# FFN weights transposed by VectorE instead of TensorE, and a new written-out order from pair 26 to the end of an attention plus FFN kernel

## The chip, the cores and the metric

The kernel runs on one core of a Trainium2 chip. Its metric is the device time of one execution in microseconds. Engines are named as in the profile: PE is TensorE's matmul stream, PEld its weight loads, DVE is VectorE, ACT is ScalarE, POOL is GpSimd, SP is SyncE, which here only issues DMAs.

## The reference, cut to what matters

A gated cross-attention layer is followed by a gated feed-forward layer (FFN), all in float32. `x` and `ctx` are 8 batches of 128 tokens with 512 features.

```
def _L0_xattn_ref(query, key, value, ...):      # 32 heads of 128, 8 k/v heads
    q = (query @ Wq) ; k = (key @ Wk) ; v = (value @ Wv)
    q = q * cos + rotate_half(q) * sin ; k = the same
    scores = einsum('bhqd,bhkd->bhqk', q, k) / sqrt(128)
    attn = softmax(where(mask == 0, -1e9, scores))
    return (attn @ v) @ Wo
def _L0_ffn_ref(x, w12, b12, w3, b3):           # w12 is 1024 x 512, w3 is 512 x 512
    x12 = einsum('bsk,mk->bsm', x, w12) + b12
    x1, x2 = split(x12, 2, axis=-1)
    return einsum('bsm,nm->bsn', silu(x1) * x2, w3) + b3
x = x + tanh(g_xattn[0]) * xattn(layernorm(x), ctx, ctx, ...)
x = x + tanh(g_ffn[0]) * ffn(layernorm(x), ...)
```

The FFN weights are stored with the contracted dimension along their rows, so they must be transposed before they can be the stationary operand of a matmul.

## The kernel before, in words

Every float32 operand of a matmul is held as two parts, `hi` (a rounded copy, written by ACT) and `lo` (the rest, written by a subtraction on DVE or POOL), and every product is three matmuls (`three`, L467 to L470). All orders are written out by hand, one list for each engine; the engines meet only by counting semaphores, and each engine runs its list strictly in order. The Python names below are those of the kernel.

After a first stage that makes keys, values and the first queries, the attention runs over 32 pairs. A pair is two units (k = 0 and 1), a unit is one batch with the four heads of one group. `n_of` numbers the units 0 to 63; unit (gg, c, k) is number 16 gg + 2 c + k, and (3, 7, 1) is the last. For a unit the work passes from engine to engine:

- PE `scores` fills the two banks `s_banks`; there is only one such set, so the scores of the next unit wait until DVE has read these (`dve_mask`).
- DVE `mask_first` and `mask_rest` add the mask and find the row minimum, ACT `exps` exponentiates, DVE `recip` inverts the row sums, POOL `norm` scales the rows.
- PE `prob_transpose` transposes the four heads into `t_bank`, ACT `pT_hi_copy` and DVE `pT_lo_split` take it out, PE `pv` multiplies with the values, ACT `o_hi_copy` and DVE `o_lo_split` take that out, PE `out_proj` multiplies with `Wo`, and DVE `add_out` adds it to `resid`.
- Beside it PE `q_block` makes the queries of coming pairs, which DVE `rot_cos` and `rot_sin` rotate and POOL `add_q` adds; ACT and POOL split weight chunks (`split_chunk`) that SP has loaded into the eight slots of `raw`.

Pairs 1 to 24 run in a hardware loop, later ones are unrolled with the same function `pair` up to pair 28 (3, 4). In `pair` the scores of a unit are issued one unit before its transposes. From pair 29 each engine has its own written-out list, because the FFN weights are prepared there. A weight tile is 128 rows of `w12` (8 tiles) or `w3` (4 tiles). For each of the 12 tiles SP loads the rows as they are, PE `ffn_tile` transposes four 128x128 blocks into `f_bank`, ACT `ffn_tile_copy` copies the bank to a stage in `t_cos` or `t_sin` and then makes the `hi` part from it, and POOL `ffn_tile_lo` makes the `lo` part. SP issues these loads after the last key and value loads (`next_unit`).

As `out_proj` of a batch's last group is added to `resid`, DVE `h_stats` takes its statistics; `inv_std_begin` and three `newton_step` give the inverse deviation of four batches at once in operations of 128x4 elements; ACT `h_norm` normalises, PE `h_tile` transposes, ACT `h_copy` and DVE `h_lo` split. PE `up(half, m)` (24 matmuls) and `down(half, b)` (12 matmuls) are the FFN. Between them ACT applies Silu and DVE and ACT gate and split the product. DVE `result` adds it up and SP stores it.

Of the kernel before, what the change touches and what calls it, by code (L numbers as in the profile page):

```python
# [13 lines left out]
GH = H // KVH  # L14
# [37 lines left out]
FFN_TILES = 12  # L52
WARM = 8
# [22 lines left out]
def build(nc, x, ctx, pos, mask, g_x, g_f, Wq, Wk, Wv, Wo, w12, b12, w3, b3, out):  # L76
# [19 lines left out]
    with es:  # L96
# [33 lines left out]
        w12_hi = cT_lo  # L130
        w12_lo = place("w12_lo", [128, KT, TOK], F32R, at["wo_hi"])
# [30 lines left out]
        up_bank = [s_banks[:, 0:512], s_banks[:, 512:1024], t_bank[:, :], pv_bank[:, :]]  # L162
# [31 lines left out]
        pe_ftile, act_fstage, act_fhi, pool_flo = sems("pe_ftile", "act_fstage", "act_fhi", "pool_flo")  # L194
# [118 lines left out]
        def h_bank(b):  # L313
            return (f_bank[0], f_bank[1], t_bank, s_banks[:, 0:512], *f_bank, *f_bank)[b]

        def ffn_tile_src(t):
            if t < RAW:
                return raw[:, t, :], raw_loaded[t], 16 * (CHUNKS // RAW + 1)
            return ffn_raw2[:, t - RAW, :], ffn_loaded[t - RAW], 16
# [8 lines left out]
        def _(sp):  # L328
# [17 lines left out]
            sp.dma_start(b12_col[:, :], b12.rearrange("(t p) -> p t", p=128), allow_slow_non_contiguous=True).then_inc(bias_loaded, 16)  # L346
# [96 lines left out]
            group_loads(KVH - 2)  # L443

            for t in range(FFN_TILES):
                dst, s, _ = ffn_tile_src(t)
# [7 lines left out]
                src = w12[t * 128:(t + 1) * 128, :] if t < 8 else w3[(t - 8) * 128:(t - 7) * 128, :]  # L454
                sp.dma_start(dst, src).then_inc(s, 16)
# [10 lines left out]
        def _(pe):  # L466
# [151 lines left out]
            def out_proj(gg, c, k):  # L618
# [7 lines left out]
                pe.wait_ge(dve_acc, n + 1)  # L626
                for h in range(GH):
                    mm = three(o_bank[k][:, :], (o_hi[:, k, h, :], o_lo[:, k, h, :]), wo_parts((c // 4) % 2, h), h == 0, h == GH - 1)
# [30 lines left out]
            def ffn_tile(t):  # L659
                src, loaded, count = ffn_tile_src(t)  # L660
                pe.wait_ge(loaded, count)
                if t < 2:
                    pe.wait_ge(dve_rot, ROTS)
                elif 8 <= t < 10:

                    tiles_done(H_T + t - 8)
                else:
                    pe.wait_ge(act_fstage, t - 1)
                transpose4(f_bank[t % 2], lambda k: src[:, k * 128:(k + 1) * 128]).then_inc(pe_ftile, 1)

# [4 lines left out]
            for c in range(1, 5):  # L675
                pair(3, c)

            def h_tile(b):
                pe.wait_ge(act_xn, B + b + 1)
                if b < 2:  # L680

                    pe.wait_ge(act_fstage, 7 + b)
                elif b == 2:
                    pe.wait_ge(act_pThi, 8 * KVH)
                    pe.wait_ge(dve_pTlo, 8 * KVH)
                elif b == 3:
                    pe.wait_ge(dve_mask, 8 * KVH)
                elif b < 6:
                    pe.wait_ge(act_fstage, FFN_TILES)
                else:  # L690
                    tiles_done(H_T + b - 2)
                transpose4(h_bank(b), lambda k: xnorm2[:, b % 4, k * 128:(k + 1) * 128]).then_inc(pe_tile, 1)

            def up(half, m):
                i = 4 * half + m
                if i >= 2:
                    pe.wait_ge(dve_gate, i - 1)
                if i == 1:

                    pe.wait_ge(act_ohi, 8 * KVH)  # L700
                    pe.wait_ge(dve_olo, 8 * KVH)
                if i == 0:
                    pe.wait_ge(act_fhi, 8)
                    pe.wait_ge(pool_flo, 8)
                for part in range(2):
                    for k in range(KT):
                        w = slice((4 * part + m) * 128, (4 * part + m + 1) * 128)
                        tk = slice(half * HT, (half + 1) * HT)
                        mm = three(up_bank[2 * (i % 2) + part], (w12_hi[:, k, w], w12_lo[:, k, w]),
# [3 lines left out]
            def down(half, b):  # L713
                n = 4 * half + b
                a_hi, a_lo = (wo1_hi, wo1_lo) if half == 0 else (act1_hi, act1_lo)
# [3 lines left out]
                if n == 0:  # L719
                    pe.wait_ge(dve_acc, 8 * KVH + 2)  # L720
# [20 lines left out]
            pv(3, 5, 1)

            out_proj(3, 5, 0)
            scores(3, 6, 1)
            ffn_tile(3)
            prob_transpose(3, 6, 0)
            out_proj(3, 5, 1)
            pv(3, 6, 0)
            prob_transpose(3, 6, 1)
            scores(3, 7, 0)  # L750
            ffn_tile(4)
            ffn_tile(5)
            pv(3, 6, 1)

            out_proj(3, 6, 0)
            scores(3, 7, 1)
            ffn_tile(6)
            prob_transpose(3, 7, 0)
            out_proj(3, 6, 1)
            pv(3, 7, 0)  # L760
            prob_transpose(3, 7, 1)
            ffn_tile(7)
            out_proj(3, 7, 0)
            pv(3, 7, 1)
            for b in range(4):
                h_tile(b)
            out_proj(3, 7, 1)
            ffn_tile(8)
            ffn_tile(9)
            tiles_done(H_T + 3)  # L770
            up(0, 0)
            ffn_tile(10)
            ffn_tile(11)
            up(0, 1)
            h_tile(4)
            h_tile(5)
            up(0, 2)
            h_tile(6)
            h_tile(7)
            up(0, 3)  # L780
            tiles_done(H_T + 7)
            up(1, 0)
            up(1, 1)
            down(0, 0)
            down(0, 1)
# [4 lines left out]
            for b in range(4):  # L790
                down(1, b)

        def ffn_tile_dst(t, part):
            if t < 8:
                return (w12_hi, w12_lo)[part][:, :, t * 128:(t + 1) * 128]
            return (wq_hi, wq_lo)[part][:, :, (t - 8) * 128:(t - 7) * 128]

        def ffn_stage(t):
            return (t_cos, t_sin)[t % 4 // 2][:, t % 2, :]

        @block.scalar
        def _(act):
# [127 lines left out]
            def ffn_tile_copy(t):  # L930
                act.wait_ge(pe_ftile, t + 1)
                if t < 2:
                    act.wait_ge(pool_rope, ROTS)
                elif t >= 4:
                    act.wait_ge(pool_flo, t - 3)
                if t == 0:
                    act.wait_ge(pe_out, 8 * (KVH - 1))
                hi(ffn_stage(t), f_bank[t % 2][:, :], act_fstage)
                act.wait_ge(act_fstage, t + 1)
                hi(ffn_tile_dst(t, 0), k4(ffn_stage(t)), act_fhi)  # L940
# [33 lines left out]
            for c in range(1, 5):  # L974
                pair(3, c)

            def h_norm(b):
# [3 lines left out]
                normalise(xnorm2[:, b % 4, :], b)  # L981
# [5 lines left out]
            def gate(half, m):  # L987
                i = 4 * half + m
                a_hi = wo1_hi if half == 0 else act1_hi
                act.wait_ge(pe_up, i + 1)  # L990
                if i < 2:
                    act.wait_ge(pool_flo, FFN_TILES - 1 + i)
                else:
                    act.wait_ge(dve_gate, i - 1)
                nc.scalar.activation(t_cos[:, i % 2, :], up_bank[2 * (i % 2)], ACT.Silu, bias=b12_col[:, m:m + 1]).then_inc(act_silu, 1)
                act.wait_ge(dve_gate, i + 1)
                if i == 0:
                    act.wait_ge(pe_out, 8 * KVH)
                hi(a_hi[:, m, :], t_sin[:, i % 2, :], act_ghi)

            q_hi_copy(3, 6, 0)
            exps(3, 5, 0)
            pT_hi_copy(3, 5, 0)
            exps(3, 5, 1)
            ffn_tile_copy(0)
            o_hi_copy(3, 5, 0)
            pT_hi_copy(3, 5, 1)
            ffn_tile_copy(1)
            o_hi_copy(3, 5, 1)
            q_hi_copy(3, 6, 1)  # L1010

            exps(3, 6, 0)
            q_hi_copy(3, 7, 0)
            ffn_tile_copy(2)
            pT_hi_copy(3, 6, 0)
            exps(3, 6, 1)
            ffn_tile_copy(3)
            o_hi_copy(3, 6, 0)
            pT_hi_copy(3, 6, 1)
            ffn_tile_copy(4)  # L1020
            o_hi_copy(3, 6, 1)
            q_hi_copy(3, 7, 1)

            exps(3, 7, 0)
            ffn_tile_copy(5)
            pT_hi_copy(3, 7, 0)
            exps(3, 7, 1)
            ffn_tile_copy(6)
            o_hi_copy(3, 7, 0)
            pT_hi_copy(3, 7, 1)  # L1030
            ffn_tile_copy(7)
            h_norm(0)
            h_norm(1)
            h_norm(2)
            o_hi_copy(3, 7, 1)
            h_norm(3)
            for b in range(4):
                h_copy(b)
            ffn_tile_copy(8)
            ffn_tile_copy(9)  # L1040
            h_norm(4)
            h_norm(5)
            ffn_tile_copy(10)
            ffn_tile_copy(11)
            act.wait_ge(bias_loaded, 16)
            gate(0, 0)
            h_norm(6)
            h_norm(7)
            h_copy(4)
            h_copy(5)  # L1050
            gate(0, 1)
            h_copy(6)
            h_copy(7)
            gate(0, 2)
            gate(0, 3)
            for m in range(4):
                gate(1, m)

        @block.gpsimd
        def _(pool):  # L1060
# [112 lines left out]
            for c in range(1, 5):  # L1173
                pair(3, c)
# [371 lines left out]
```

## Time and profile before

| | us |
|---|---|
| median of 3 runs (674.37 to 674.54) | 674.37 |
| the profiled execution's own time | 674.48 |
| its span in the profile | 672.7 |
| PE busy | 661.8 (98%) |
| DVE busy | 482.4 (72%) |
| POOL busy | 385.6 (57%) |
| ACT busy | 322.0 (48%) |

The span runs from the first to the last instruction; 1.8 us of the profiled execution lie around it. PE's busy time counts overlapping matmuls once, and each matmul is shown for longer than the distance to the next one, so idle time on PE is read best from the distances between starts. The clock line of the profile shows full speed in all 40 slices.

### The profile page before, as it was taken

Reading aid. Unit: us, or ns where it says so; the run is one execution under the profiler, and the core shown is the slowest. Engines: PE = TensorE matmul, PEld = TensorE weight load, DVE = VectorE, ACT = ScalarE, POOL = GpSimd, SP = SyncE. Lnnn points to the kernel's source line nnn. Section 1 sums busy time; section 2 is a strip of 40 time slices with the busy share of each in tenths; the row PEclk is TensorE's granted clock in tenths of the full one; section 3 lists DMA queues with packets and bytes.
Section 4 is the critical chain, followed back from the end, with each engine's and each line's share of the span. In section 5 each row is a group of like instructions: output and inputs, shape, how many; then the busy total and the mean of one; then the engine's idle time right before and its main releaser. Section 6 shows DMA issues by size and latency. Waiting matters only on the chain.

```text
span 672.7 us, 11338 instructions
## 1 busy us (share of the span) xinstructions
PE 661.8 (98%) x3357; PEld 554.3 (82%) x3357; DVE 482.4 (72%) x1223; ACT 322.0 (48%) x903; POOL 385.6 (57%) x323
## 2 busy tenths in 40 slices
PE   8999999999999999999999999999999999999998
PEld 7888888788888888888888888888888887778886
DVE  3987666877777777777777777777777777774433
ACT  4336613554554544554554544554554537756210
POOL 6457757966666666656666666556666655631000
PEclk9999999999999999999999999999999999999999
DMA  9996982331213121321212120321211142000002
GB/s 304 317 318 215 304 295 94 142 100 58 95 39 104 32 94 33 109 71 55 94 43 98 33 94 31 110 79 45 78 33 31 32 157 80 0 1 1 1 31 95
DMA packets 62157, 66.34 MB, mean 99 GB/s; under 512 B 5920, under 2 KB 43808, under 8 KB 62112
## 3 DMA queue, kind: packets, MB, share of 16 engines
q1 hardware_dynamic: 60688, 64.77, 29.5%
q0 software_dynamic: 384, 1.05, 0.4%
q8 instruction: 18, 0.29, 0.2%
q14 instruction: 27, 0.22, 0.1%
q10 hardware_dynamic: 1040, 0.00, 0.1%
HBM read 46.93 MB, written 18.87 MB: 98 GB/s over the span
## 4 chain that ended last, share of the span: by engine, by line
PE 90%; DVE 4%; ACT 2%; issue 1%; POOL 1%; DMA 1%; SPq 0%; DVEq 0%; ACTq 0%
PE f_bank L468 11%; PE f_bank L470 11%; PE f_bank L469 11%; PE o_bank L468 9%; PE o_bank L470 9%; PE o_bank L469 9%; PE s_banks L591 6%; PE t_bank L474 4%; PE pv_bank L468 4%; PE pv_bank L470 3%; PE pv_bank L469 3%; PE s_banks L592 2%; PE t_bank L468 1%; PE t_bank L470 1%; PE t_bank L469 1%
## 5 line engine op out<-in xcount | busy, mean ns | idle before, releaser
L1114 POOL TENSOR_TENSOR prob<-prob,small 128x512 f32<-128x512 f32 x64 | 66.7, 1042 | 134.5 <-DVE small L1356 134.5
L876 ACT ACTIVATE prob<-prob,small 128x128 f32<-128x128 f32 x256 | 99.8, 391 | 80.3 <-DVE small L1346 74.9
L468 PE MATMUL o_bank<-wo_hi,o_hi 128*128 128x512 f32 x256 | 105.7, 413 | 0.0
L806 ACT ACTIVATE o_hi<-pv_bank 128x512 fp32r<-128x512 f32 x64 | 38.4, 599 | 138.1 <-PE pv_bank L470 137.7
L468 PE MATMUL f_bank<-xT_hi,wq_hi 128*128 128x512 f32 x256 | 101.5, 396 | 0.0
L470 PE MATMUL o_bank<-wo_hi,o_lo 128*128 128x512 f32 x256 | 100.5, 393 | 0.0
L469 PE MATMUL o_bank<-wo_lo,o_hi 128*128 128x512 f32 x256 | 100.0, 391 | 0.0
L1072 POOL TENSOR_TENSOR q_lo<-q,q_hi 128x512 fp32r<-128x512 f32 x64 | 82.7, 1292 | 30.0 <-ACT q_hi L806 30.0
L470 PE MATMUL f_bank<-xT_hi,wq_lo 128*128 128x512 f32 x256 | 99.8, 390 | 0.0
L469 PE MATMUL f_bank<-xT_lo,wq_hi 128*128 128x512 f32 x256 | 99.8, 390 | 0.0
L1258 DVE TENSOR_TENSOR t_sin<-f_bank,rope 64x512 f32<-64x512 f32 x128 | 88.2, 689 | 2.8
L1105 POOL TENSOR_TENSOR q<-t_cos,t_sin 128x512 f32<-128x512 f32 x64 | 82.9, 1295 | 1.0 <-DVE t_sin L1258 0.9
L1258 DVE TENSOR_TENSOR t_cos<-f_bank,rope 128x512 f32<-128x512 f32 x64 | 43.9, 687 | 32.1 <-PE f_bank L470 32.0
L1346 DVE CUSTOM_DVE_ANT_0 prob<-s_banks,prob 128x128 f32<-128x128 f32 x256 | 59.2, 287 | 10.2 <-DVE prob L1337 7.1
L591 PE MATMUL s_banks<-k_parts,q_hi 128*128 128x256 f32 x256 | 63.0, 324 | 0.7 <-issue 0.4
L1370 DVE SCALAR_TENSOR_TENSOR resid<-o_bank,small,resid 128x512 f32<-128x512 f32 x64 | 47.9, 749 | 19.6 <-PE o_bank L470 18.6
L1211 DVE TENSOR_TENSOR o_lo<-pv_bank,o_hi 128x512 fp32r<-128x512 f32 x64 | 44.1, 689 | 20.9 <-ACT o_hi L806 20.8
L470 PEld LDWEIGHTS o_bank<-wo_hi,o_lo 128*128 128x128 f32 x256 | 48.0, 188 | 11.0
L592 PE MATMUL s_banks<-k_parts,q_lo 128*128 128x128 f32 x256 | 56.9, 222 | 0.0
L470 PEld LDWEIGHTS f_bank<-xT_hi,wq_lo 128*128 128x128 f32 x256 | 48.0, 188 | 10.2
L468 PEld LDWEIGHTS f_bank<-xT_hi,wq_hi 128*128 128x128 f32 x256 | 48.1, 188 | 9.5 <-issue 0.4
L469 PEld LDWEIGHTS f_bank<-xT_lo,wq_hi 128*128 128x128 f32 x256 | 48.2, 188 | 9.1
(176 smaller groups left out, 1463.3 us busy)
## 6 DMA issues: line engine op xcount, KB each, us to landing
k_scratch<-ks_parts SPq DMA_DIRECT2D x16, 512.0 KB, 3.2
raw<-in_L_xattn_Wq_dram SPq DMA_DIRECT2D x32, 256.0 KB, 2.7
raw<-in_L_xattn_Wo_dram SPq DMA_DIRECT2D x32, 256.0 KB, 2.7
k_parts<-k_scratch SPq DMA_DIRECT2D x16, 512.0 KB, 3.7
v_scratch<-vs_hi SPq DMA_DIRECT2D x16, 256.0 KB, 3.9
v_scratch<-vs_lo SPq DMA_DIRECT2D x16, 256.0 KB, 3.9
v_hi<-v_scratch SPq DMA_DIRECT2D x16, 256.0 KB, 3.9
v_lo<-v_scratch SPq DMA_DIRECT2D x16, 256.0 KB, 4.4
```

The source lines that it names most:

```text
L468: nc.tensor.matmul(dst, st[0], mv_[0], start=start, stop=False)
L469: nc.tensor.matmul(dst, st[0], mv_[1], start=False, stop=False)
L470: return nc.tensor.matmul(dst, st[1], mv_[0], start=False, stop=stop)
L591: nc.tensor.matmul(s_banks[:, 256 * h:256 * (h + 1)], q_hi[:, k, h, :], k_parts[:, half, b, :], start=True, stop=False)
L592: mm = nc.tensor.matmul(s_banks[:, 256 * h:256 * h + 128], q_lo[:, k, h, :], k_parts[:, half, b, 0:128], start=False, stop=True)
L876: e = nc.scalar.activation(prob[:, k, h, :], prob[:, k, h, :], ACT.Exp, bias=nmin[k][:, h:h + 1], scale=-1.0, accum_out=psum_row[k][:, h:h ...
L1072: nc.gpsimd.tensor_tensor(dst, a, b_, ALU.subtract).then_inc(s, 1)
L1105: nc.gpsimd.tensor_tensor(q32[:, (e // 4) % 2, e % 4, :], t_cos[:, ts, :], t_sin[:, ts, :], ALU.add).then_inc(pool_rope, 1)
L1114: nc.gpsimd.tensor_tensor(prob[:, k], prob[:, k], rrow[k].unsqueeze(2).to_broadcast([128, GH, S]), ALU.mult).then_inc(pool_norm, 1)
L1258: return nc.vector.tensor_tensor(dst, a, b_, ALU.mult)
L1346: op = nc.vector.tensor_tensor_reduce(prob[:, k, h, :], s_parts[:, h, 0, :], prob[:, k, h, :], 1.0, HUGE, ALU.add, ALU.min, nmin[k][:, h:h ...
L1370: nc.vector.scalar_tensor_tensor(out=resid[:, b, :], in0=o_bank[k][:, :], scalar=tg_x, in1=resid[:, b, :], op0=ALU.mult, op1=ALU.add).then ...
```

## The change

1. SP loads each FFN weight tile in four DMAs of 32 partitions each, in runs of 128 elements, so that blocks of 32x32 lie where one DVE `transpose` of a 128x512 tile, which transposes each block of 32x32, gives the wanted layout. The order of the contracted features is thereby permuted, and `h_norm` writes the normalised rows in the same permuted order. PE's `ffn_tile` goes, and of ACT's two copies for a tile one (`ffn_hi`) stays, reading the transposed tile.
2. From pair 26 DVE, ACT and POOL have lists of their own (before: from pair 29), PE from pair 27. The scores of a unit are issued about a pair ahead of its transposes.
3. SP issues the first three weight tiles before the loads of group 7's first keys and values, five more before its second, four after them. The bias `b12` is loaded late, in eight DMAs, and no longer in the first stage.
4. The two output projections of pair 30 go to `f_bank`, and the FFN's `up` blocks to `f_bank` and `s_banks`. The last tiles' splits stand between FFN blocks, each `up` of the first half waits only for its own two weight tiles, and the last lists interleave differently.

In the diff `ffn_tile` is in DVE's program, `ffn_hi` in ACT's and `ffn_lo` in POOL's.

```diff
+LATE = 3
-        w12_hi = cT_lo
-        w12_lo = place("w12_lo", [128, KT, TOK], F32R, at["wo_hi"])
+        w12_hi = place("w12_hi", [128, RAW, KT, 128], F32R, at["raw"])
+        w12_lo = place("w12_lo", [128, RAW, KT, 128], F32R, at["cT_lo"])
+        w12_all = place("w12_all", [128, RAW, KT, 128], F32, at["cT_lo"])
+        w3_all = place("w3_all", [128, KT, E], F32, at["wq_lo"])
...
-        up_bank = [s_banks[:, 0:512], s_banks[:, 512:1024], t_bank[:, :], pv_bank[:, :]]
+        up_bank = [f_bank[0][:, :], f_bank[1][:, :], s_banks[:, 0:512], s_banks[:, 512:1024]]
...
+        def bank_of_out(gg, c, k):
+            return f_bank[k] if isinstance(gg, int) and 8 * gg + c == PAIRS - 2 else o_bank[k]
+        def ffn_src(t, i):
+            f = slice(128 * i, 128 * i + 128)
+            if t < RAW:
+                return w12.rearrange("(h j m b) f -> h m b j f", h=2, j=4, m=4)[t % 2, t // 2, :, :, f]
+            return w3.rearrange("(t j b) f -> t b j f", t=4, j=4)[t - RAW, :, :, f]
...
-            group_loads(KVH - 2)
-                sp.dma_start(dst, src).then_inc(s, 16)
+                for i in range(4):
+                    sp.dma_start(dst[32 * i:32 * i + 32, :].rearrange("b (j f) -> b j f", j=4), ffn_src(t, i)).then_inc(s, 16)
+            for t in range(3):
+                ffn_load(t)
+            next_unit(0, KVH - 1)
+            for t in range(3, RAW):
+                ffn_load(t)
+            next_unit(1, KVH - 1)
+            for t in range(RAW, FFN_TILES):
+                ffn_load(t)
...
+            def ffn_tile(t):
+                src, loaded, count = ffn_raw(t)
+                dve.wait_ge(loaded, count)
+                if t == RAW:
+                    dve.wait_ge(pe_kq, ROTS)
+                nc.vector.transpose(ffn_f32(t).rearrange("p k (j b) -> p k j b", j=4), src.rearrange("p (j k a) -> p k j a", j=4, k=4)).then_inc(dve_ftile, 1)
+            def ffn_hi(t):
+                act.wait_ge(dve_ftile, t + 1)
+                hi(ffn_parts(t)[0], ffn_f32(t), act_fhi)
+            def ffn_lo(t):
+                pool.wait_ge(act_fhi, t + 1)
+                minus(ffn_parts(t)[1], ffn_f32(t), f32(ffn_parts(t)[0]), pool_flo)
```

PE's list from pair 27 (after), with T for `prob_transpose`, q for `q_block`, and the unit as c,k: q12, scores 3,1, q13, T 3,0, scores 4,0, out 2,0, scores 4,1, T 3,1, pv 3,0, q14, out 2,1, scores 5,0, T 4,0, q15, pv 3,1, scores 5,1, T 4,1, out 3,0, pv 4,0, out 3,1, T 5,0, scores 6,0, pv 4,1, out 4,0, scores 6,1, T 5,1, pv 5,0, out 4,1, scores 7,0, T 6,0, pv 5,1, out 5,0, scores 7,1, T 6,1, pv 6,0, out 5,1, T 7,0, pv 6,1, out 6,0, T 7,1, pv 7,0, out 6,1, h_tile 0, pv 7,1, h_tile 1, out 7,0, h_tile 2, h_tile 3, out 7,1, up 0,0, up 0,1, h_tile 4 to 6, up 0,2, h_tile 7, up 0,3, up 1,0 to up 1,2, down 0,0, up 1,3, down 0,1 to down 1,3.

DVE's list at the end of the attention (after): ..., o_lo 6,0, h_stats 2, add_out 5,1, pT_lo 7,0, recip 7,1, h_stats 3, o_lo 6,1, inv_std_begin, three newton_step, shifts, pT_lo 7,1, o_lo 7,0, add_out 6,0, h_lo 0, ffn_tile 7, h_lo 1, o_lo 7,1, add_out 6,1, h_lo 2, h_lo 3, ... POOL's (after): ..., norm 7,0, norm 7,1, ffn_lo 4 to ffn_lo 11 with nothing between them. ACT's (after): ..., o_hi 6,1, o_hi 7,0, pT_hi 7,1, h_norm 0, h_norm 1, h_copy 0, h_norm 2, o_hi 7,1, ...

## Rows read from the trace of the kernel before

**Rows 1.** The page: busy times, and the chain by engine.
```profile
PE 661.8 (98%) x3357; PEld 554.3 (82%) x3357; DVE 482.4 (72%) x1223; ACT 322.0 (48%) x903; POOL 385.6 (57%) x323
PE 90%; DVE 4%; ACT 2%; issue 1%; POOL 1%; DMA 1%; SPq 0%; DVEq 0%; ACTq 0%
```
**Rows 2.** Busy us and count of each engine by stretch; clock, DMA share, GB/s.
```profile
510.55:555.80 45.25, 45.25 (x235) 38.30 (x234) 34.77 (x97) 21.11 (x69) 25.96 (x22) 1.00 0.25 84
555.80:600.00 44.20, 40.78 (x227) 32.97 (x226) 31.84 (x105) 32.93 (x89) 21.54 (x19) 1.00 0.08 28
```
**Rows 3.** PE in order of time, start and length, pair 27 to the end.
```profile
525.64 0.39 PE L468 MATMUL f_bank<-xT_hi,wq_hi 128*128 128x512 f32 x1
...
555.82 0.39 PE L468 MATMUL o_bank<-wo_hi,o_hi 128*128 128x512 f32 x1
...
558.54 0.28 PE L591 MATMUL s_banks<-k_parts,q_hi 128*128 128x256 f32 x1
...
559.41 0.61 PE L474 MATMUL f_bank<-ident,raw 128*128 128x128 f32 x4
...
576.90 0.66 PE L474 MATMUL t_bank<-ident,prob 128*128 128x128 f32 x4 [0.66 <-POOL prob L1114]
...
578.26 1.06 PE L474 MATMUL f_bank<-ident,raw 128*128 128x128 f32 x8
579.07 0.47 PE L468 MATMUL pv_bank<-pT_hi,v_hi 128*128 128x512 f32 x1
579.38 0.40 PE L469 MATMUL pv_bank<-pT_lo,v_hi 128*128 128x512 f32 x1
...
669.05 0.39 PE L470 MATMUL o_bank<-wq_hi,act_lo 128*128 128x512 f32 x1
```
**Rows 4.** The transposes of the first 8 FFN tiles on PE: count, busy, mean ns.
```profile
L474 PE MATMUL f_bank<-ident,raw 128*128 128x128 f32 x32 | 4.6, 275 | 0.0
```
**Rows 5.** DVE's last mask operation before pair 26; then unit (3, 6, 1) on DVE and POOL.
```profile
511.54 0.28 DVE L1346 CUSTOM_DVE_ANT_0 prob<-s_banks,prob 128x128 f32<-128x128 f32 x1
...
571.93 0.69 DVE L1337 TENSOR_TENSOR prob<-s_banks,mfill 128x512 f32<-128x512 f32 x1 [0.42 <-PE s_banks L592]
575.80 1.04 POOL L1114 TENSOR_TENSOR prob<-prob,small 128x512 f32<-128x512 f32 x1 [1.29 <-DVE small L1356]
```
**Rows 6.** DVE and ACT operations grouped by shape: count, busy us, mean ns.
```profile
L1214 DVE BATCH_NORM_STATS2 small<-resid 128x6 f32<-128x512 f32 x16 | 11.0, 690 | 0.3
L1233 DVE SCALAR_TENSOR_TENSOR small<-small 128x4 f32<-128x4 f32 x6 | 1.0, 163 | 0.2
L876 ACT ACTIVATE prob<-prob,small 128x128 f32<-128x128 f32 x256 | 99.8, 391 | 80.3 <-DVE small L1346 74.9 <-issue 5.3
L806 ACT ACTIVATE o_hi<-pv_bank 128x512 fp32r<-128x512 f32 x64 | 38.4, 599 | 138.1 <-PE pv_bank L470 137.7 <-DMA k_scratch<-ks_parts 0.3
```
**Rows 7.** SP's queue around the FFN loads; the last two rows: KB each, median us to landing.
```profile
529.43 0.33 SPq L374 DMA_DIRECT2D k_parts<-k_scratch  x1
541.83 3.78 SPq L455 DMA_DIRECT2D raw<-in_L_ffn_w_dram  x8
k_parts<-k_scratch SPq DMA_DIRECT2D x16, 512.0 KB, 3.7
raw<-in_L_ffn_w_dram SPq DMA_DIRECT2D x8, 256.0 KB, 4.6
```
**Rows 8.** Newton steps on DVE beside POOL subtractions, twice.
```profile
42.62 1.18 DVE L1231 SCALAR_TENSOR_TENSOR small<-small 128x8 f32<-128x8 f32 x1
43.84 1.21 DVE L1232 TENSOR_TENSOR small<-small 128x8 f32<-128x8 f32 x1
...
43.74 1.28 POOL L1072 TENSOR_TENSOR wk_lo<-raw,wk_hi 128x512 fp32r<-128x512 f32 x1
...
591.72 1.14 DVE L1232 TENSOR_TENSOR small<-small 128x4 f32<-128x4 f32 x1
...
591.54 1.31 POOL L1072 TENSOR_TENSOR w_lo<-t_sin,cT_lo 128x512 fp32r<-128x512 f32 x1 [1.34 <-ACT cT_lo L806]
```

More of the change, by code:

```diff
@@ L674, in _ @@
                     pair(gg, c)
-            for c in range(1, 5):
+            for c in range(1, LATE):
                 pair(3, c)
@@ L765, in _ @@
[L765 to L766 removed]
+            h_tile(2)
+            h_tile(3)
             out_proj(3, 7, 1)
[L768 to L770 removed]
             up(0, 0)
[L772 to L773 removed]
             up(0, 1)
@@ L776, in _ @@
             h_tile(5)
+            h_tile(6)
             up(0, 2)
-            h_tile(6)
             h_tile(7)
             up(0, 3)
-            tiles_done(H_T + 7)
             up(1, 0)
             up(1, 1)
+            up(1, 2)
             down(0, 0)
+            up(1, 3)
             down(0, 1)
-            up(1, 2)
-            up(1, 3)
             down(0, 2)
             down(0, 3)
[L790 to L799, printed above, removed]
+            down(1, 0)
+            down(1, 1)
+            down(1, 2)
+            down(1, 3)
         @block.scalar
@@ L973, in _ @@
                     pair(gg, c)
-            for c in range(1, 5):
-                pair(3, c)
+            pair(3, 1)
             def h_norm(b):
@@ L1033, in _ @@
             h_norm(1)
+            h_copy(0)
             h_norm(2)
             o_hi_copy(3, 7, 1)
+            h_copy(1)
             h_norm(3)
[L1037 to L1040, printed above, removed]
+            h_copy(2)
+            h_copy(3)
+            silu(0)
             h_norm(4)
             h_norm(5)
[L1043 to L1046, printed above, removed]
+            ffn_hi(7)
@@ L1049, in _ @@
             h_copy(4)
+            silu(1)
+            gated_hi(0)
+            ffn_hi(8)
             h_copy(5)
-            gate(0, 1)
             h_copy(6)
+            silu(2)
+            ffn_hi(9)
             h_copy(7)
[L1054 to L1057, printed above, removed]
+            ffn_hi(10)
+            silu(3)
+            gated_hi(1)
+            ffn_hi(11)
+            gated_hi(2)
+            silu(4)
+            gated_hi(3)
+            silu(5)
+            gated_hi(4)
+            silu(6)
+            gated_hi(5)
+            silu(7)
+            gated_hi(6)
+            gated_hi(7)
         @block.gpsimd
@@ new lines, in _ @@
+            add_out(3, 1, 0)
+            ffn_tile(3)
+            mask_scores(3, 3, 0)
+            ffn_tile(4)
+            add_out(3, 1, 1)
+            recip(3, 3, 0)
+            cos_q(3, 12)
+            mask_scores(3, 3, 1)
+            sin_q(12)
+            mask_scores(3, 4, 0)
+            recip(3, 3, 1)
+            pT_lo_split(3, 3, 0)
+            o_lo_split(3, 2, 1)
+            cos_q(3, 13)
+            recip(3, 4, 0)
+            sin_q(13)
+            ffn_tile(5)
+            mask_scores(3, 4, 1)
@@ new lines, in _ @@
+            newton_step(0, 4, NEWTON_OPS, 2)
+            shifts(0, 4)
+            pT_lo_split(3, 7, 1)
+            o_lo_split(3, 7, 0)
+            add_out(3, 6, 0)
+            h_lo(0)
+            ffn_tile(7)
+            h_lo(1)
+            o_lo_split(3, 7, 1)
+            add_out(3, 6, 1)
+            h_lo(2)
+            h_lo(3)
+            h_stats(4)
+            add_out(3, 7, 0)
+            h_stats(5)
+            add_out(3, 7, 1)
+            h_stats(6)
+            h_stats(7)
+            inv_std_begin(4, 8, 2 * NEWTON_OPS)
@@ L1517, in _ @@
-            gate(1, 3)
-            for n in range(2, 8):
-                result(n)
+            bias3(6)
+            bias3(7)
+            gated_lo(7)
+            result(2)
+            result(3)
+            result(4)
+            result(5)
+            result(6)
+            result(7)
 _INS = ['x', 'ctx_4096', 'pos_BxS2', 'mask_BxSxS2_ik0', 'g_xattn', 'g_ffn', 'L0_xattn_Wq', 'L0_xattn_Wk', 'L0_xattn_Wv',
```

462 lines of the change are left out of this document (282 added, 180 removed).

## The prediction, made blind

> **What bounds the kernel now.** I read the page first. PE is busy 98% of the span, and the chain of work that ended last is 90% PE [rows 1]. The stretches come next: PE has no idle time in pairs 26 to 28 (510.55 to 555.8), while DVE is busy 34.8 of 45.3 us there and POOL 26.0; between 555.8 and 600, the written-out end of the attention, PE is busy 40.8 of 44.2 us [rows 2]. So only two things can pay: less work on PE, anywhere, and less waiting of PE behind 555.8.
>
> How much waiting there is I take from distances between starts on PE [rows 3]. Twelve matmuls take 2.72 (555.82 to 558.54), so one is 0.2267. A unit's scores take 0.87 (558.54 to 559.41), with the later start of what follows 0.93. Eight transposes take 0.81 (578.26 to 579.07) and make the next matmul 0.31 long instead of 0.23: 0.89, or 0.445 for four. From 555.82 to the last issue's end, 669.05 + 0.23 = 669.28, are 113.5 us. In them lie 402 matmuls (8 output projections and 8 `down` of 12, 6 `pv` of 3, 8 `up` of 24): 91.1; five scores: 4.65; 26 blocks of four transposes (6 of probabilities, 8 of rows, 12 of FFN weights): 11.6. The sum is 107.4, so PE stands still for 6.1 us. What it waits for is the softmax: unit (3, 6, 1) goes from DVE's mask at 571.93 by ACT's exponentials to POOL's scaling, 575.80 to 576.84, and PE's transposes, which had nothing else in front of them, start at 576.90, released by POOL [rows 3, 5].
>
> **The change part by part.** *PE's FFN transposes.* 48 go, 32 of them in the row shown and 16 of `w3` like them [rows 4], 12 blocks of 0.445 = 5.3 us. They stand in PE's own order and nothing hides them, so this is gained in full if nothing takes its place.
>
> *Scores a pair ahead.* This can take out the 6.1 us of waiting, if the other engines deliver by then. I walked the new orders by hand from PE's 525.64 and DVE's 511.8 [rows 3, 5] with the lengths above and these, a little under the lengths shown since successive operations overlap: a DVE operation on 128x512 0.62 (0.69 shown, [rows 5, 6]), a unit's mask work 1.8 (one such, a wait of 0.2, four of 128x128), a pair of sine products 1.35, exponentials of a unit 1.55 (four of 0.39), an ACT copy 0.54 (0.60) [rows 6], POOL's scaling 1.0 and its other operations 1.26 [rows 5, 8], 0.05 for a hand-over, and a matmul's result visible 0.17 after its issue. The walk finds no wait of PE up to unit (7, 0). Some joins, as wanted by PE and ready: transposes (3,0) 532.0 and 529.75; scores (4,1) 536.15 and 535.4; `pv` (4,1) 557.45 and 556.8; transposes (5,1) 561.8 and 561.3; transposes (7,0) 575.2 and 575.05; transposes (7,1) 579.05 and 578.5. ACT has late places (exponentials (5,0) stand behind `o_hi` (3,1) until 549.25), but the pair of lead covers them. So stall-free PE would issue its last attention matmul at 669.28 − 5.3 − 6.1 = 657.9 less the FFN's 288 x 0.2267 = 65.3 and four `h_tile` of 0.445: 590.8.
>
> *A new wait.* At the end of the attention DVE's Newton steps meet POOL's weight subtractions. Their cost is shown twice [rows 8]: 0.16 us operations took 1.18 and 1.21 beside two back-to-back POOL subtractions, the first followed by the second at 43.74 and this one ending at 45.02, and 1.14 beside the one that ended at 592.85; each came free as POOL's ended. The first two also show that a DVE operation gets in between two POOL ones and the next one waits again. In the new order: exponentials of (7,1) end at 575.4; DVE comes to its reciprocal at 577.3 (after `o_lo` (6,0), statistics 2, `add_out` (5,1), `pT_lo` (7,0)); POOL scales from 577.5 to 578.5 and then has `ffn_lo` 4, 5 and 6 ready, whose `hi` parts are old: to 579.8, 581.05 and 582.3. DVE, after statistics 3 and `o_lo` (6,1), begins the inverse deviation at 579.0. Two operations with one input pass, the next three wait for one POOL end each, to 582.3, and the seven left at 0.2 end at 583.75, instead of 581.4. `h_norm` 0 ends at 584.55. PE wants `h_tile` 0 at 590.8 − 7.9 = 582.9 (behind it stand `pv`, two projections and three `h_tile`, 7.9 with its own 0.445) and gets it at 584.6; `pv` (7,1) and all else are queued behind it. The next joins (`pv` 585.05 wanted, 584.95 ready; `h_tile` 1 585.75, 585.3; `h_tile` 2 and 3 with 0.9 or more to spare) are met, so 1.75 us stay: the attention ends at 592.55. Bounds: 0 if they don't block, 3 if a fourth operation is caught and the two late joins slip.
> The Trainium skill's page "SBUF — State Buffer", in its section on who interferes with whom, says that a VectorE instruction with two SBUF inputs contends with a GpSimd instruction that reads SBUF, and that the later one blocks until the other is done. The trace agrees, by the 1.14 us at 591.72 of an operation form that takes 0.16 otherwise; without this rule and the rows the sum would be 1.75 us lower.
>
> *DVE's transposes.* No row shows one. The nearest by size and inputs is the statistics operation, one SBUF input, 128x512, 0.69 [rows 6], and I take that: 12 x 0.62 = 7.4 us on DVE, seven of them in the attention, on an engine that is a quarter idle there [rows 2]. The low end is a single 128x128 operation's 0.28 [rows 5]. The high end is four partition groups one after another, 2.8. At 0.28 nothing changes for PE; at 1.1 each I find at most 0.5 us late at the join of (7,0); at 2.8 it is a rival below. ACT loses one of two copies for a tile, 12 x 0.6 [rows 6], which pays only through the joins.
> The Trainium skill's page "VectorE: DVE Perf Modes", section "The three transpose paths", has 311 ns for a 128x128 bf16 transpose on VectorE against 390 on TensorE. Were each of the four blocks of a tile to cost that, a tile would be an estimated 1.24 us, and PE would be late by the half microsecond just named.
>
> *SP and the loads.* 48 load DMAs take the place of 12, at 0.47 each to issue (3.78 for 8, [rows 7]); `b12` adds eight. Landing took 4.6 us [rows 7], in runs four times as long as the new ones; I allow 4 to 10. Tiles 0 to 2 are issued by 497 (their slots are free with pair 24), long before DVE wants tile 0 at 511.9. Tiles 3 to 7 wait for their slots, the last for POOL's `split_chunk` of pair 27, which the walk has at 545.15. Queued behind it are group 7's second keys, before issued at 529.43 [rows 7], now at 547; PE wants them at 556.5 for scores (6,0): 5.9 us to spare behind a landing of 3.7 [rows 7]. Cost nothing, or up to 4 if they land as slowly as 10 + 3.7. `b12` out of the first stage gains 0 to 0.2, since no one there waits for what was queued behind it.
>
> *The FFN.* With `up` (0,0) at 592.55, DVE finishes the second four batches' inverse deviation at 598.9 (POOL is idle by then, waiting for ACT's `hi` of tile 7), tiles 8 and 9 and the first gate at 602; PE wants that gate after two `up` of 5.44 and three `h_tile`, at 604.8. The later gates and splits have 1.5 us or more. `down` (1,0) is wanted 56 us after 592.55 and its last operand is ready at 54 even with `result` (1) before it. So 67.1 us of PE work run dense, and after the last issue 672.7 − 669.28 = 3.4 us pass as before.
>
> **Sum.** 674.48 − 5.3 − 6.1 + 1.75 = 664.85 for a profiled execution. The median before is 0.1 below its profiled execution, and the two joins with under 0.2 to spare will cost some 0.1 or 0.2: I forecast 664.9.
>
> **The rivals.** (A) The Newton steps aren't held, because POOL runs later than walked or its subtractions start between them: 663.1. For it: my POOL times are rough; against: the subtractions are queued right behind a scaling that itself waits for DVE, 1.6 us ahead of the steps, so they overlap by construction. (B) Joins slip: the orders are strict, with six joins under 0.7 us, and each slip of DVE or ACT is passed on to the next unit. Two or three slips of 0.5 to 1 us give 666 to 668, say 667. For it: the present written-out part loses 6.1 us in just this manner, from orders that look sound. Against: the lead of a pair. (C) A transpose costs 1.4 to 2.8 us. At 2.8, seven in the attention add 14.7 us; DVE's idle time in my walk there is some 9, so 6 come through, and with the first gate 1 us late: 672. (D) Slower than before: the transpose runs block by block. A tile is 16 columns of blocks on each of 4 partition groups; at a small operation's 0.16 [rows 6] per block, 64 blocks one by one are 10.3 us, and seven tiles add 67, less 9 idle: some 58 us of which 9.6 are saved elsewhere, about 722. It decides from where the added time exceeds 9 + 9.6 over seven tiles, 3.4 us for a transpose. Nothing in the trace speaks for it but that no row excludes it.
>
> **How the numbers follow.** Forecast 0.50, its own range 664.0 to 666.2; (A) 0.15; (B) 0.25; (C) 0.06; (D) 0.04. The range of 8 in 10 goes from just under A, 662.6, to the upper part of B, 668.5. This kernel's measurement tells 0.2%, 1.3 us, from no change. All but parts of (C) and (D) are faster by more: 0.95; a hundredth of each of these two is within: 0.02; slower 0.03.
>
> **What would show it.** Right: no transposes of weights on PE; from 525 to 575 PE's stretches full; a 128x512 DVE transpose of 0.6 to 0.75; Newton operations of about 0.4, 1.2 and 1.2 us beside POOL's `ffn_lo`, and one PE gap of 1.5 to 2 us before `h_tile` 0; no gap in the FFN. Wrong: gaps before probability transposes at (4,x) to (6,x) (B), Newton operations all at 0.16 (A), transposes above 1.2 (C, D), or scores (6,0) waiting for a DMA. The forecast is wrong as a whole if the gap before `h_tile` 0 is absent or PE waits elsewhere for more than 1.5 us.

## The result, and the profile after

| | before | after |
|---|---|---|
| median, us | 674.37 (674.07 to 674.54, 4 runs) | 664.98 (664.75 to 665.09, 4 runs) |
| profiled execution, us | 674.48 | 664.75 |
| span, us | 672.7 | 662.9 |

The ratio is 0.986 (95% interval 0.9848 to 0.9872). The forecast was 664.9, the range 662.6 to 668.5.

The page of the changed kernel, busy times and the chain, to be held against [rows 1]:
```profile
PE 654.6 (99%) x3309; PEld 550.3 (83%) x3309; DVE 490.2 (74%) x1235; ACT 314.1 (47%) x891; POOL 385.5 (58%) x323
PE 94%; DVE 2%; DMA 1%; issue 1%; POOL 0%; ACT 0%; DVEq 0%
```
PE has its 48 instructions fewer, DVE 12 more, ACT 12 fewer. DVE's and ACT's share of the chain has gone from 6% to 2% and PE's from 90% to 94%: less of the time is now spent in steps that PE waits for.

The changed kernel by stretch (columns as in [rows 2]), the second stretch ending where stall-free PE was to end the attention:
```profile
510.55:555.80 45.25, 45.25 (x242) 38.64 (x241) 39.55 (x119) 27.21 (x92) 30.42 (x26) 1.00 0.29 82
555.80:590.80 35.00, 33.14 (x182) 28.01 (x181) 30.93 (x87) 21.73 (x60) 15.23 (x13) 1.00 0.07 16
590.80:662.90 72.10, 68.88 (x312) 56.85 (x310) 35.21 (x63) 18.24 (x30) 6.88 (x5) 1.00 0.08 30
```
In the first stretch DVE is 39.55 us busy where it was 34.77 in [rows 2], and PE still has no idle time. In the second PE lacks 1.86 us, all in one place; the 3.2 us that it lacks in the third lie after its last matmul.

PE in order of time, that place first, then the start of the FFN and the last matmul:
```profile
582.09 0.39 PE L511 MATMUL f_bank<-wo_hi,o_lo 128*128 128x512 f32 x1
584.34 0.66 PE L515 MATMUL s_banks<-ident,xnorm 128*128 128x128 f32 x4 [1.86 <-ACT xnorm L1009]
...
592.39 0.39 PE L509 MATMUL f_bank<-xT_hi,w_hi 128*128 128x512 f32 x1
...
659.29 0.39 PE L511 MATMUL o_bank<-wq_hi,act_lo 128*128 128x512 f32 x1
```
Read by distances, the gap before `h_tile` 0 is 584.34 - 582.09 - 0.23 = 2.02 us. From 500 to the last matmul no other distance between starts is more than 0.14 us above a stall-free one; before, PE stood still behind 555.8 for 6.1 us by the sum in the prediction. PE's view of waits for the same stretch has one line:
```profile
PE s_banks L515 <- ACT xnorm L1009: 1.9, 1, 1.9
```

What held `h_norm` 0 back, on DVE and then POOL, in order of time:
```profile
577.61 0.69 DVE L1306 TENSOR_TENSOR o_lo<-pv_bank,o_hi 128x512 fp32r<-128x512 f32 x1
578.22 0.95 DVE L1320 TENSOR_SCALAR small<-small 128x4 f32<-128x4 f32 x1
579.20 1.22 DVE L1321 TENSOR_SCALAR small<-small 128x4 int32<-128x4 int32 x1
580.45 1.21 DVE L1326 SCALAR_TENSOR_TENSOR small<-small 128x4 f32<-128x4 f32 x1
581.70 0.16 DVE L1327 TENSOR_TENSOR small<-small 128x4 f32<-128x4 f32 x1
...
583.27 0.16 DVE L1336 SCALAR_TENSOR_TENSOR small<-small 128x4 f32<-128x4 f32 x1
...
577.86 3.79 POOL L1143 TENSOR_TENSOR w_lo<-w_all,w_hi 128x512 fp32r<-128x512 f32 x3
```
Three operations took 0.95, 1.22 and 1.21 us instead of 0.16. POOL's three subtractions end at about 579.1, 580.4 and 581.65 (3.79 in thirds), and at each of these ends one DVE operation comes free and the next is caught. `o_lo`, which reads PSUM and SBUF, took its usual 0.69, but it had started 0.25 us ahead of the first subtraction; one that starts inside a subtraction is shown in the experiments.

DVE's transposes, grouped (count, busy us, mean ns, idle before), and the DMAs that feed them (KB each, median us to landing):
```profile
L1532 DVE STREAM_TRANSPOSE w_all<-raw 128x512 f32<-128x512 f32 x8 | 5.5, 700 | 0.0
L1532 DVE STREAM_TRANSPOSE w_all<-ffn_raw 128x512 f32<-128x512 f32 x4 | 2.6, 685 | 0.0
...
raw<-in_L_ffn_w_dram SPq DMA_DIRECT2D x32, 64.0 KB, 2.0
ffn_raw<-in_L_ffn_w_dram SPq DMA_DIRECT2D x16, 64.0 KB, 2.4
```
The single ones took 662 to 711 ns, as long as a statistics operation of that size [rows 6].

### The profile page after: what moved, and what is told of

It is laid out like the page before. It is cut to its first block, busy times and chain, and to the rows that moved or that the text cites. A ratio compares the mean times of both kernels' runs of the same rounds, so it can differ in the third digit from the quotient of the medians.

```text
span 662.9 us, 11265 instructions
## 1 busy us (share of the span) xinstructions
PE 654.6 (99%) x3309; PEld 550.3 (83%) x3309; DVE 490.2 (74%) x1235; ACT 314.1 (47%) x891; POOL 385.5 (58%) x323
## 4 chain that ended last, share of the span: by engine, by line
PE 94%; DVE 2%; DMA 1%; issue 1%; POOL 0%; ACT 0%; DVEq 0%
PE f_bank L509 12%; PE f_bank L511 12%; PE f_bank L510 12%; PE o_bank L509 10%; PE o_bank L511 10%; PE o_bank L510 10%; PE s_banks L632 6%; PE t_bank L515 4%; PE pv_bank L509 3%; PE pv_bank L511 3%; PE pv_bank L510 3%; PE s_banks L633 2%; PE t_bank L511 1%; PE t_bank L509 1%; PE s_banks L511 1%; PE s_banks L510 1%
## 5 line engine op out<-in xcount | busy, mean ns | idle before, releaser
L509 PE MATMUL o_bank<-wo_hi,o_hi 128*128 128x512 f32 x248 | 102.1, 412 | 0.0
L511 PE MATMUL o_bank<-wo_hi,o_lo 128*128 128x512 f32 x248 | 97.4, 393 | 0.0
L510 PE MATMUL o_bank<-wo_lo,o_hi 128*128 128x512 f32 x248 | 96.9, 391 | 0.0
L1465 DVE SCALAR_TENSOR_TENSOR resid<-o_bank,small,resid 128x512 f32<-128x512 f32 x62 | 46.4, 748 | 17.4 <-PE o_bank L511 16.2
L511 PEld LDWEIGHTS o_bank<-wo_hi,o_lo 128*128 128x128 f32 x248 | 46.6, 188 | 10.6
```

The source lines that it names most:

```text
L509: nc.tensor.matmul(dst, st[0], mv_[0], start=start, stop=False)
L510: nc.tensor.matmul(dst, st[0], mv_[1], start=False, stop=False)
L511: return nc.tensor.matmul(dst, st[1], mv_[0], start=False, stop=stop)
L1465: nc.vector.scalar_tensor_tensor(out=resid[:, b, :], in0=bank_of_out(gg, c, k)[:, :], scalar=tg_x, in1=resid[:, b, :], op0=ALU.mult, op1=A ...
```

## The experiments

Each group was run with the kernel before on the same chip (674.47 and 674.42 in the two groups).

**The hold, taken away in two ways.** First the three subtractions go ahead of the last two scalings, where POOL has time:

```diff
-            norm(3, 7, 0)
-            norm(3, 7, 1)
             ffn_lo(4)
             ffn_lo(5)
             ffn_lo(6)
+            norm(3, 7, 0)
+            norm(3, 7, 1)
```


> The changed kernel (664.98 us median, span 662.9) with POOL's ffn_lo 4, 5 and 6 moved in front of the scaling of unit (3, 7, 0), into POOL's idle 4.42 us before 573.40. Theory L (DVE's small operations are held while a POOL subtraction runs): all 12 operations of the first inverse deviation last 0.16 to 0.17 us, the 2.0 us gap of PE before h_tile 0 goes, span 660.9 to 661.2, time about 663.0. Rival O (the inverse deviation is late because of its place in DVE's order, or the engine is slow there for another reason): the three long operations stay and the time stays at 665. Rival M (the moved subtractions make the scaling of (7, 0) late): a new gap on PE before its transposes, above 0.5 us, and 663.5 to 665.

Then they stay where they are, but begin only when the shift operations are done:

```diff
             norm(3, 7, 1)
+            pool.wait_ge(dve_shift, 2)
             ffn_lo(4)
```


> The changed kernel with one wait more: POOL begins ffn_lo 4 only when DVE has done the first four batches' inverse deviation (dve_shift at 2). It takes away the overlap with nothing moved earlier. Theory L: the same gain as with the early place, span about 661, time about 663.0, with POOL's three subtractions behind 581. Rival O: 665. If the subtractions now hold DVE's later operations of two SBUF inputs instead, none of which is on the way to the first FFN block, the time doesn't show it.

Measured: 663.03 (662.75 to 663.06, ratio 0.9829, interval 0.9816 to 0.9843) and 663.09 (662.97 to 663.24, ratio 0.9831, 0.9817 to 0.9844). DVE in the first, the first and the third of the small operations, and the last:
```profile
578.38 0.16 DVE L1320 TENSOR_SCALAR small<-small 128x4 f32<-128x4 f32 x1
...
578.78 0.16 DVE L1326 SCALAR_TENSOR_TENSOR small<-small 128x4 f32<-128x4 f32 x1
...
580.55 0.16 DVE L1336 SCALAR_TENSOR_TENSOR small<-small 128x4 f32<-128x4 f32 x1
```
The second run, in which the subtractions start just behind the last step and a split from PSUM and SBUF (`pT_lo`) runs beside them:
```profile
578.67 0.16 DVE L1321 TENSOR_SCALAR small<-small 128x4 f32<-128x4 f32 x1
...
580.84 0.17 DVE L1337 SCALAR_TENSOR_TENSOR small<-small 128x4 f32<-128x4 f32 x1
581.38 0.69 DVE L1307 TENSOR_TENSOR pT_lo<-t_bank,pT_hi 128x512 fp32r<-128x512 f32 x1 [0.37 <-ACT pT_hi L843]
...
581.08 3.80 POOL L1143 TENSOR_TENSOR w_lo<-w_all,w_hi 128x512 fp32r<-128x512 f32 x3 [2.73 <-DVE small L1337]
```
In both, PE waits for nothing from 500 to its last matmul. Both times are 1.9 us below the changed kernel's, as large as its gap (2.02). The hold is the cause of the gap: it goes with an earlier as well as with a later start of POOL's work. The `pT_lo` that starts 0.3 us into the first subtraction still takes 0.69: this form isn't held.

**The first stage's bias load, put back.** Pair 26 began 0.37 us earlier than before (its first load of values at 510.38, before 510.75). Is that `b12`, which no longer stands ahead of the mask?

```diff
+            for h in range(2):
+                for i in range(4):
+                    sp.dma_start(b12_col[32 * i:32 * i + 32, 4 * h:4 * h + 4], ...)
             sp.dma_start(mask_raw[:, :, :], mask.rearrange("b q k -> q b k")).then_inc(mask_loaded, 16)
```
(and the same eight taken out behind the last FFN load)

> The changed kernel with the eight b12 loads back in the first stage, ahead of the mask load. In the changed kernel all of pair 26 stands 0.36 us earlier than in the kernel before. If the b12 load made this 0.36 us, the span is 663.2 to 663.4 and pair 26 begins as before; if not (another layout of the program or of its instruction loads), it stays at 662.9. In my prediction I gave this edit 0 to 0.2 us. The time alone, 665.0 or 665.4, can hardly tell; the trace can.

Measured: 665.82 (664.88 to 666.54, four runs; ratio 0.9867, interval 0.9852 to 0.9882). The load of values starts at 510.45. But the same load starts at 510.83, 510.66 and 510.55 in three other kernels whose first stage is the changed one's, and at 510.49 in one with the first stage of before: executions differ by up to 0.45 us here. So no effect of `b12` can be told, and the 0.37 isn't shown to be anything but scatter. The four times are 664.88, 665.24, 666.39 and 666.54. The profiled one was among the long ones, and its stretches of 2 us across and behind PE's gap show why (columns as in [rows 2]):
```profile
582.00:584.00 2.00, 0.55 (x3) 0.13 (x1) 1.76 (x9) 0.46 (x1) 0.00 (x0) 1.00 0.00 0
...
586.00:588.00 2.00, 2.00 (x8) 1.62 (x7) 1.64 (x3) 2.00 (x4) 0.00 (x0) 0.50 0.00 0
588.00:590.00 2.00, 2.00 (x8) 1.59 (x7) 1.35 (x3) 0.07 (x1) 0.00 (x0) 0.69 0.03 8
```
and two of its matmuls inside them:
```profile
586.70 0.63 PE L510 MATMUL o_bank<-wo_lo,o_hi 128*128 128x512 f32 x1
...
589.25 0.39 PE L510 MATMUL o_bank<-wo_lo,o_hi 128*128 128x512 f32 x1
```
The granted clock, third from the end, is 0.50 in the stretch 586 to 588, which is 1.2 of 2.4 GHz, after PE had stood still from 582.4 to 584.4. Seven matmuls from 586.13 to 589.25 take 3.1 us instead of some 1.6: about 1.5 us, the distance of the two long times from the two short. The granted clock over the whole execution was 0.997 in both long ones and 0.999 and 1.0 in the short ones; in the profiled execution of the changed kernel it is 1.00 across the same gap. So in this execution the gap cost its length and some 1.5 us on top. Five other profiled executions (the changed kernel's and those of the next experiments with the new order) have a gap of 1.85 to 2.5 us at this place and 1.00 behind it. Why the clock fell in one and not in the others stays open, and that the second long time has the same cause is read only from its time and its mean clock.

**The transposing work, put back on PE.** The new order with 12 spare blocks of four transposes of the identity, 8 behind scores and `pv` between scores (6,0) and `pv` (6,0), 4 between the last `up` and `down`:

```diff
+            def spare(bank, wait=False):
+                if wait:
+                    pe.wait_ge(dve_rot, ROTS)
+                transpose4(bank, lambda k: ident[:, :])
...
             scores(3, 6, 0)
+            spare(f_bank[0], True)
             pv(3, 4, 1)
+            spare(f_bank[1], False)
```


> The changed kernel with 12 blocks of four PE transposes that nothing reads, put back at about their old density: eight between the units of pairs 28 to 30, four in the FFN. By my sum a block costs 0.445 us wherever PE is full: +5.3 us, span about 668.2, time about 670.3, with the gap before h_tile 0 still there at about 2 us. Rival: as in the kernel before, part of them falls into time in which PE would wait anyway (the 2.0 us gap) and the cost is 3.3 us or less, 668.3; that needs DVE's chain to the inverse deviation not to be pushed along by PE.

Measured: 670.34 (670.19 to 670.82, ratio 0.994, interval 0.9925 to 0.9955), 5.36 us above the changed kernel, 0.447 for a block. The gap is there, 1.85 us by distances against 2.02:
```profile
585.92 0.39 PE L511 MATMUL f_bank<-wo_hi,o_lo 128*128 128x512 f32 x1
588.00 0.66 PE L515 MATMUL s_banks<-ident,xnorm 128*128 128x128 f32 x4 [1.69 <-ACT xnorm L1026]
```

**The transposing work, taken from PE in the old order.** The kernel before without `ffn_tile` on PE; ACT copies the raw rows, so the FFN's weights stay untransposed:

```diff
             scores(3, 5, 1)
-            ffn_tile(0)
             prob_transpose(3, 5, 0)
...
-                act.wait_ge(pe_ftile, t + 1)
+                src, loaded, count = ffn_tile_src(t)
+                act.wait_ge(loaded, count)
...
-                hi(ffn_stage(t), f_bank[t % 2][:, :], act_fstage)
+                hi(ffn_stage(t), src, act_fstage)
```


> The kernel before with the 12 blocks of PE transposes of FFN weights left out and nothing else moved; ACT copies the untransposed tile from raw instead of from the bank, so the FFN is computed with weights that are not transposed. It parts the two halves of the gain. If both add up as in my sum, the transposes alone bring the full 5.3 us: 669.1, and PE still stands still for about 6 us. Rival F (the transposes fill time in which PE waits for a softmax anyway): those in front of a wait, tiles 0, 7 and partly the pairs, bring nothing; then PE's waiting grows by 2 to 3 us and the time is 671 to 672, and the new order is worth more than the 6.1 us that I gave it, 8 to 9.

Measured: 673.6 (673.4 to 673.87, ten runs; ratio 0.9989, interval 0.9979 to 0.9998). 5.3 us of work were taken from PE, and 0.8 came out at the end (0.1 to 1.4 by the interval), less than either expectation. PE's waits from 555 on in this kernel (us in total, times, longest), first lines:
```profile
PE t_bank L474 <- POOL prob L1103: 2.9, 6, 0.9
PE pv_bank L468 <- issue: 1.2, 2, 0.6
PE s_banks L468 <- DVE t_sin L1480: 0.8, 1, 0.8
```
And the same view of the kernel before, first line:
```profile
PE t_bank L474 <- POOL prob L1114: 2.0, 4, 0.7
```
PE's first and last matmul behind 555.5 in the kernel without the blocks:
```profile
555.55 0.39 PE L468 MATMUL o_bank<-wo_hi,o_hi 128*128 128x512 f32 x1
...
667.97 0.39 PE L470 MATMUL o_bank<-wq_hi,act_lo 128*128 128x512 f32 x1
```
By the sum of the prediction, now with 14 blocks instead of 26, 102.0 us of work lie in these 112.65, so PE stands still for 10.6 us instead of 6.1. The blocks had stood in time in which PE would have waited: without them PE arrives sooner and waits longer. Most of the growth is at the softmax and what follows it (the lines of `t_bank` and `pv_bank`); some 1.6 us of it lie in the FFN, ahead of `up` (0,0) and of `up` (0,2), the latter waiting for the first gate (the 0.8), where four of the twelve blocks had stood.

**How much room DVE has.** Each of the 12 DVE transposes done twice, and four times, one after another:

```diff
+                nc.vector.transpose(ffn_f32(t)..., src...).then_inc(dve_twice, 1)
+                dve.wait_ge(dve_twice, t + 1)
                 nc.vector.transpose(ffn_f32(t)..., src...).then_inc(dve_ftile, 1)
```


> The changed kernel with every DVE transpose of a weight tile done twice, one behind the other: 1.3 us for a tile instead of 0.65, 12 times. By the walk of my prediction PE is at most 0.5 us late for it (DVE has about 9 us of idle time in front of the last unit): 665.0 to 665.5. Rival J (the joins have no slack and each late DVE operation is passed on): 7 x 0.65 = 4.5 us more, 669.5.

> The changed kernel with every DVE transpose done four times, 2.6 us for a tile: rival C of my prediction at its full price. There I had seven tiles adding some 14 us less 9 us of idle time and 1 us at the first gate, 672 us, 7 above the changed kernel. If the slack isn't where the tiles are, more: up to 14 + 5, 684.

Measured: twice 665.36 (665.2 to 666.06, ratio 0.987, interval 0.9854 to 0.9887), 0.4 above the changed kernel, with two new gaps on PE of 0.19 and 0.15. Four times 677.14 (676.97 to 677.82, ratio 1.0044, interval 1.003 to 1.0059), 12.2 above it and slower than the kernel before. The latter's waits on PE from 500 on, the two of `pv`:
```profile
PE pv_bank L510 <- issue: 3.5, 1, 3.5
...
PE pv_bank L510 <- DVE o_lo L1307: 1.5, 1, 1.5
```
its stretch from 511 to 540, and 2 us behind its longest wait:
```profile
511.00:540.00 29.00, 23.92 (x113) 18.84 (x112) 27.71 (x72) 11.58 (x38) 13.49 (x12) 0.94 0.20 55
...
525.00:527.00 2.00, 2.00 (x8) 1.70 (x7) 1.94 (x4) 0.56 (x2) 1.06 (x2) 0.50 0.00 0
```
and the longest wait in order of time, DVE's first and last of eight transposes and what follows, then PE:
```profile
517.48 0.71 DVE L1533 STREAM_TRANSPOSE w_all<-raw 128x512 f32<-128x512 f32 x1
...
522.54 0.71 DVE L1539 STREAM_TRANSPOSE w_all<-raw 128x512 f32<-128x512 f32 x1
523.18 0.65 DVE L1307 TENSOR_TENSOR pT_lo<-t_bank,pT_hi 128x512 fp32r<-128x512 f32 x1
...
520.05 0.39 PE L512 MATMUL o_bank<-wo_hi,o_lo 128*128 128x512 f32 x1
523.93 0.77 PE L510 MATMUL pv_bank<-pT_hi,v_hi 128*128 128x512 f32 x1 [3.50 <-issue]
```
Two tiles stand one behind the other in DVE's list, so eight transposes, 5.7 us, are in front of the `pT_lo` that `pv` needs. The profile names no releaser ("issue"), but `pv` starts as soon as that split is written. DVE, third of the busy times, is 27.71 of 29 us busy between 511 and 540, and PE only 23.92. After this pause of 3.65 us the granted clock is down too: 0.50 from 525 to 527, and the first matmul takes 0.77.

**Which operations are held.** Ahead of the Newton steps three pairs of spare operations, on 128x4 elements as they are:

```diff
+            for i in range(3):
+                nc.vector.reciprocal(small[:, 96 + 8 * i:100 + 8 * i], rstd[:, 0:4])
+                nc.vector.tensor_scalar(small[:, 100 + 8 * i:104 + 8 * i], rstd[:, 0:4], 1.0, None, ALU.add)
             inv_std_begin(0, 4, NEWTON_OPS)
```


> The changed kernel with six more DVE operations of 128x4 in front of the first inverse deviation, where POOL's three subtractions run: three times a reciprocal and a tensor_scalar, each with one SBUF input, results unused. It asks which forms are held. In the changed kernel two tensor_scalar operations with one input were held (0.95 and 1.22 us), against my prediction that one input passes. If every operation on DVE is held, the reciprocals take the long times too; if it is a matter of form, all three reciprocals last 0.17 and the tensor_scalars beside POOL last to the end of a POOL subtraction each. Either way the inverse deviation itself then runs free, and the time is within 1 us of 665.

Measured: 665.43 (one run). DVE, then POOL:
```profile
578.49 0.17 DVE L1639 RECIPROCAL small<-small 128x4 f32<-128x4 f32 x1
578.58 0.87 DVE L1640 TENSOR_SCALAR small<-small 128x4 f32<-128x4 f32 x1
579.36 0.17 DVE L1639 RECIPROCAL small<-small 128x4 f32<-128x4 f32 x1
579.45 1.25 DVE L1640 TENSOR_SCALAR small<-small 128x4 f32<-128x4 f32 x1
580.61 0.17 DVE L1639 RECIPROCAL small<-small 128x4 f32<-128x4 f32 x1
580.70 1.25 DVE L1640 TENSOR_SCALAR small<-small 128x4 f32<-128x4 f32 x1
581.86 0.15 DVE L1320 TENSOR_SCALAR small<-small 128x4 f32<-128x4 f32 x1
...
578.13 3.79 POOL L1143 TENSOR_TENSOR w_lo<-w_all,w_hi 128x512 fp32r<-128x512 f32 x3
```
All six read one SBUF tile of 128x4. The reciprocals pass in 0.17 each, the `tensor_scalar`s are held to the end of a subtraction, and the Newton steps then run free, since POOL has finished. Only the first reciprocal lies wholly inside a subtraction, the other two start as one ends; but none of the changed kernel's 64 reciprocals took more than 0.181 us. How many operations are held follows the number of POOL's subtractions: three here and in the changed kernel, two and one in [rows 8].

## Why the prediction came out right, and which steps of it did not

| | with 12 blocks of transposes on PE | without them |
|---|---|---|
| old order | 674.37 | 673.6 |
| new order, with the hold | 670.34 | 664.98 |
| new order, without it | not run | 663.03 |

**"This is gained in full if nothing takes its place."** As a price of a block when PE is full, right: 0.447 against 0.445. As a term of its own, mis-sized: in the old order it is 0.8, not 5.3, because PE would have waited in the time that the blocks took, and "nothing hides them" looked only at PE's list. The second term holds with the blocks in place: all of the change but their removal brought 4.0 us (674.37 to 670.34) and left the hold's 1.9, together 6.0 of the 6.1 forecast (a sum, since that kernel without the hold wasn't run). The sum 11.4 held since both were removed at once (674.37 to 663.03 is 11.3). How the 11.3 is shared depends on which edit comes first: 0.8 and 10.6, or 6.0 and 5.4.

**Scores a pair ahead.** The walk found no wait before unit (7, 0), and there was none to the end of the attention but the forecast one. Transposes (7,0) were wanted at 575.2 and started at 574.59, (7,1) at 579.05 and 578.45, each 0.6 early, 0.37 of it because pair 26 began earlier. Rival B fails: no join slipped, and the 0.1 or 0.2 allowed for two of them wasn't needed.

**The new wait.** Three operations held and an `h_tile` 0 late by 2.02 us, against three and 1.75. The reading of which three was wrong: "two operations with one input pass". The two with one input, both `tensor_scalar`, were held; instead of numbers three to five it was the first three. It came out nearly alike because POOL has three subtractions there and each end frees one; that is luck for this step. But now nine operations of 0.2 stood behind POOL's last end and not seven: from there to the last of them 1.78 us passed (581.65 to 583.43) instead of 1.45, about what the gap is longer than forecast. The trace of the kernel before had already shown that this form is held: a `tensor_scalar` with one input took 0.33 us, twice its usual time, and ended at 604.58, as the second of two POOL subtractions ended at 604.55:
```profile
604.25 0.33 DVE L1225 TENSOR_SCALAR small<-small 128x4 f32<-128x4 f32 x1
...
602.00 2.55 POOL L1072 TENSOR_TENSOR wq_lo<-t_cos,wq_hi 128x512 fp32r<-128x512 f32 x2 [9.15 <-ACT wq_hi L806]
```
The Trainium skill's page "SBUF — State Buffer", in the section on who interferes with whom, counts among the contenders not only operations with two SBUF inputs but also the faster modes that a `tensor_scalar` can enter; here the trace agrees as to who is held, with 0.87 and 1.25 us beside reciprocals of 0.17; that these operations ran in such a mode no run shows. Rival A (663.1) was the right price of its absence: 663.03.

**DVE's transposes.** 0.685 to 0.700 us, as taken (0.69), nothing on PE's path. The estimate of 1.24, worked out from the figure for a 128x128 bf16 transpose in the Trainium skill's page "VectorE: DVE Perf Modes", section "The three transpose paths", isn't what they cost. "At 1.1 each at most 0.5 us late" stands against 0.4 at 1.4. Rival C's price was too low: at 2.8 it forecast 672, and at some 2.9 (four, one after another) 677.14 was measured. Its step "DVE's idle time in my walk there is some 9" failed: the idle time is spread over some 65 us, while in that run five of the seven tiles stand between 511 and 540, two of them next to each other, and each join pays for what is in front of it; the lower clock behind the pause comes on top. So rival D's threshold of 3.4 us a transpose is also too high: the change turns slower before 2.9.

**The rest.** Pair 26 started 0.37 early. The first `up` was due at 592.55 and started at 592.39: 0.37 early, 0.27 more gap, and 0.06 unaccounted for. Group 7's second keys were issued at 546.65 (547), no one waited for them; the small loads landed in 2.0 to 2.4 us (4 to 10 allowed). The FFN took 67.13 us of PE (67.1), 3.38 us passed after the last issue (3.4), and 1.85 lay around the span (1.8).

That the profiled execution came within 0.1 us of the sum (664.75 against 664.85) is in part luck: the early start of 0.37 and the gap's extra 0.27 have opposite signs.

The version with POOL's subtractions earlier beats both kernels: 663.03 us, 1.7% below before.

## What to carry to other kernels

Work in a strict list can be nearly free though its engine is 98% busy, if it stands in front of a wait: before a removed instruction is counted, ask when what comes behind it is ready. Two edits, one that takes work away and one that shortens waits, are priced together and not one by one. Cover on an engine is counted in the stretch between two joins, not over a stage. And what another engine has queued at the moment when a latency chain of tiny operations runs is part of that chain: three subtractions moved by some 9 us gave 1.9 us.

## What the runs showed of the hardware that was not expected

- DVE beside POOL's 128x512 subtractions: held are operations on 128x4 with two SBUF inputs and `tensor_scalar` with one, f32 and int32 (0.87 to 1.25 us for 0.16); not held are `reciprocal` (0.17) and the subtraction from PSUM and SBUF (0.69, started inside one).
- A 128x512 float32 `transpose` in blocks of 32x32 is one DVE operation of 0.66 to 0.71 us.
- After a 2.0 us pause of PE the granted clock was at its lower level for some 3 us in the profiled execution of one kernel, though behind pauses of 1.85 to 2.5 us at the same place it stayed at 1.00 in those of five others; behind one of 3.65 us it was at 0.50 again.
